# First scan of a state-space layer: two of three products with C computed by GpSimd, with their rows of C copied by ScalarE

## The reference, cut to what matters

```python
def step(h, inp):
    xt, dtt, Bt, Ct = inp
    dA = jnp.exp(dtt[:, :, None] * A)
    h = h * dA + (dtt * xt)[:, :, None] * Bt[:, None, :]
    y = jnp.einsum('bdn,bn->bd', h, Ct) + xt * D
    return (h, y)
h0 = jnp.zeros((B_, D_MODEL, D_STATE), x.dtype)
...
_, ys = jax.lax.scan(step, h0, xs)
```

## Time and profile before

| What | us |
|---|---|
| median of three runs (3369.27 to 3370.46) | 3370.19 |
| the profiled execution, its own time | 3370.55 |
| its span, first to last instruction | 3368.8 |
| VectorE busy in the span (73%) | 2445.5 |
| TensorE matmuls busy (82%) | 2766.3 |
| ScalarE busy (40%) | 1341.0 |
| GpSimd busy (18%) | 621.7 |

### The profile page before, as it was taken

One profiled execution on the slowest core, in us unless ns is written; L12 is line 12 of the kernel. 1 busy time (PEld: TensorE's weight loads), 2 busy tenths in 40 slices (PEclk: granted clock), 3 DMA queues, 4 the chain that ended last, 5 costly groups with the idle time before them and its releaser, 6 DMA issues.

```text
span 3368.8 us, 37353 instructions
## 1 busy us (share of the span) xinstructions
PE 2766.3 (82%) x12264; PEld 1579.4 (47%) x12264; DVE 2445.5 (73%) x4932; ACT 1341.0 (40%) x2454; POOL 621.7 (18%) x426
## 2 busy tenths in 40 slices
PE   4226989997898997888997989980359999999998
PEld 2003754444764444764445754440126656566564
DVE  6996687997587997687996684017767676776766
ACT  2323316763326773325772316544441131311313
POOL 2443000332100332100333000001000040310404
PEclk9558899998899998989998899995669999999999
DMA  5001000101000001000001000105010000000000
GB/s 157 0 0 45 1 1 7 26 17 52 1 1 7 23 20 53 1 1 7 23 20 52 1 1 13 26 17 118 0 33 1 1 13 1 1 13 1 14 1 13
DMA packets 57628, 65.88 MB, mean 20 GB/s; under 512 B 27756, under 2 KB 46689, under 8 KB 56801
## 3 DMA queue, kind: packets, MB, share of 16 engines
q1 hardware_dynamic: 57441, 63.51, 7.0%
HBM read 45.22 MB, written 9.88 MB: 16 GB/s over the span
## 4 chain that ended last, share of the span: by engine, by line
PE 58%; DVE 26%; issue 5%; ACT 4%; POOL 2%; DMA 1%; DVEq 1%; SPq 1%; POOLq 0%; ACTq 0%
PE psum L1713 13%; PE psum L383 8%; DVE arena L543 6%; PE psum L938 4%; PE psum L790 3%; PE psum L1773 3%; PE psum L1052 3%; DVE arena L538 3%; PE psum L956 2%; PE psum L770 2%; PE psum L373 2%; PE psum L374 2%; PE psum L269 2%; PE psum L781 2%; DVE z_both L1439 1%
## 5 line engine op out<-in xcount | busy, mean ns | idle before, releaser
L1713 PE MATMUL psum<-weights,arena 128*128 128x384 f16 x3072 | 535.3, 329 | 3.9 <-DVE arena L2069 2.9
L383 PE MATMUL psum<-arena,weights 128*128 128x512 f32 (+1 forms) x1024 | 522.6, 593 | 4.9 <-ACT arena L457 4.9
L457 ACT ACTIVATE arena<-psum,minus_scale 128x512 f32<-128x512 f32 x512 | 350.3, 685 | 215.5 <-PE psum L383 213.7
L2072 DVE SCALAR_TENSOR_TENSOR arena<-psum,arena 128x384 f32<-128x384 f32 x480 | 295.8, 616 | 193.0 <-PE psum L1713 182.6
L1713 PEld LDWEIGHTS psum<-weights,arena 128*128 128x128 f16 x3072 | 304.3, 99 | 193.3 <-issue 8.6
L598 POOL TENSOR_TENSOR arena<-arena 128x1024 f32<-128x1024 f32 x128 | 273.8, 2139 | 598.8 <-DVE arena L543 598.2
L543 DVE TENSOR_TENSOR_SCAN arena<-weights,arena 128x1026 f32<-128x1026 f32 x128 | 293.9, 2296 | 18.4 <-ACT weights L450 3.8
L246 POOL TENSOR_SCALAR shifted<-mean_var 128x4 f32<-128x4 f32 x40 | 9.7, 244 | 1313.4 <-DVE mean_var L223 1313.4
L1948 POOL TENSOR_TENSOR arena<-arena 128x512 f32<-128x512 f32 x112 | 147.5, 1320 | 510.0 <-ACT arena L1887 499.3
L383 PEld LDWEIGHTS psum<-arena,weights 128*128 128x128 f32 (+1 forms) x1024 | 166.0, 163 | 98.8 <-ACT arena L457 12.1
L450 ACT ACTIVATE weights<-arena,weights 128x512 f32<-128x512 f32 x256 | 169.2, 712 | 102.8 <-DVE arena L543 102.8
(11 more groups left out here) (322 smaller groups left out, 4880.8 us busy)
## 6 DMA issues: line engine op xcount, KB each, us to landing
arena<-arena SPq DMA_DIRECT2D x64, 128.0 KB, 2.3
arena<-head_inv SPq DMA_DIRECT2D x32, 256.0 KB, 3.4
weights<-in_qkv SPq DMA_DIRECT2D x2, 3072.0 KB, 17.4
weights<-gate_upT_kept SPq DMA_DIRECT2D x4, 1408.0 KB, 6.4
x_all<-in_x SPq DMA_DIRECT2D x4, 1024.0 KB, 12.0
weights<-in_cWkv SPq DMA_DIRECT2D x4, 1024.0 KB, 11.3
out<-x_all SPq DMA_DIRECT2D x4, 1024.0 KB, 4.4
weights<-downT_kept SPq DMA_DIRECT2D x4, 640.0 KB, 7.1
```

The lines of the kernel that those rows point to most:

```text
L383: pe.matmul(psum[0:rows, 3 + turn % 2, :], value_and_ones(kt, hd), expd[:, i % 2, :], start=kt == 0, stop=kt == NT - 1).then_inc(pv2_done, 1)
L457: a.activation(expd[:, i % 2, :], psum[:, i % 3, :], ACT.Exp, bias=minus_scale[:, :], scale=SCALE / QK ** 2).then_inc(exp_done, 1)
L1713: last = pe.matmul(psum[:, n % PROJ_BANKS, 0:W3], zT_parts[:, of_z, c, k * P:(k + 1) * P], w_parts[:, c, e, of_w, :], start=c == 0 and j == 0,
L2072: step_ = v.scalar_tensor_tensor(qkv[:, k, :], src, router_w[:, k, e:e + 1], qkv[:, k, :], ALU.mult, ALU.add)
```

## The change

In the first scan alone, 20 of the 32 products with C move from VectorE to GpSimd: those of the steps j below 30 for which j is not a multiple of 3. ScalarE copies each such row of C from PSUM into one of three SBUF buffers (`c_rows`, `keep_c`); GpSimd multiplies the state by it in place, both inputs in SBUF, and then adds (L636 and L644 of the new kernel). GpSimd no longer waits for the recurrence of the next step in the first scan. The rows of B get PSUM banks 0 to 2, the rows of C banks 3 to 7. In the loop's scans everything stays as it was. The core of the diff:

```diff
+        def b_bank(j, alone):
+            return j % 3 if alone else 5 + 2 * j % 3
+
+        def c_bank(j, alone):
+            return 3 + j % 5 if alone else 5 + (2 * j + 1) % 3
+
+        def by_pool(j, alone):
+
+            return alone and j % 3 != 0 and j < STEPS - 2
+
+        def products(upto, alone):
+
+            of_pool = sum(by_pool(j, alone) for j in range(upto))
+            return upto - of_pool, of_pool
...
-        def spread_b(pe, j):
+        def spread_b(pe, j, alone):
...
-            if j >= 2:
+            if alone and j >= 3:
+                pe.wait_ge(w_done, j - 2)
+            if not alone and j >= 2:
                 pe.wait_ge(p_done, j - 1)
...
-            if j >= 1:
+            if alone and j >= 5:
+                of_dve, of_pool = products(j - 4, alone)
+                pe.wait_ge(p_done, of_dve)
+                if of_pool:
+                    pe.wait_ge(c_row_kept, of_pool)
+            if not alone and j >= 1:
                 pe.wait_ge(w_done, j)
...
+        def keep_c(a, j):
+            i = products(j, True)[1]
+            a.wait_ge(c_psum, j + 1)
+            if i >= 3:
+                a.wait_ge(p_pool_done, i - 2)
+            a.activation(c_rows[:, i % 3, :], psum[:, c_bank(j, True), :], ACT.Copy).then_inc(c_row_kept, 1)
...
+                    if q == 0 and by_pool(j, not heads):
+                        keep_c(a, j)
...
-            v.wait_ge(c_psum, j + 1)
-            v.tensor_tensor(to[:, :, 1:], to[:, :, 1:], both(5 + (2 * j + 1) % 3), ALU.mult).then_inc(p_done, 1)
+            if not by_pool(j, alone):
+                v.wait_ge(c_psum, j + 1)
+                v.tensor_tensor(to[:, :, 1:], to[:, :, 1:], both(c_bank(j, alone)), ALU.mult).then_inc(p_done, 1)
...
-                g.wait_ge(p_done, j + 1)
-                if j + 1 < STEPS:
+                of_dve, of_pool = products(j + 1, not heads)
+                if by_pool(j, not heads):
+                    to = h[:, j % RING, :, 1:]
+                    g.wait_ge(scan_done, j + 1)
+                    if half == 0:
+                        g.wait_ge(end_kept, j + 1)
+                    g.wait_ge(c_row_kept, of_pool)
+                    row = c_rows[:, (of_pool - 1) % 3, :].unsqueeze(1).to_broadcast([P, 2, HALF])
+                    g.tensor_tensor(to, to, row, ALU.mult).then_inc(p_pool_done, 1)
+                    g.wait_ge(p_pool_done, of_pool)
+                else:
+                    g.wait_ge(p_done, of_dve)
+                if heads and j + 1 < STEPS:
                     g.wait_ge(scan_done, j + 2)
```

More of the change, by code:

```diff
@@ L207, in program @@
         Norm = namedtuple("Norm", "stat mean_var rstd shifted stats_ready shifted_ready rstd_ready")
+        p_pool_done, c_row_kept = exp_done, o_kept
         by_stage = Norm(stat, mean_var, rstd, shifted, stats_ready, shifted_ready, rstd_ready)
@@ L293, in program @@
         soft = r.take(DC, T)
+        c_rows = r.take(3, HALF)
         r = Region(arena, scan_end)
@@ L353, in spread_b, with spread_c @@
                 pe.wait_ge(split_ready, 1)
-            if j >= 2:
+            if alone and j >= 3:
+                pe.wait_ge(w_done, j - 2)
+            if not alone and j >= 2:
                 pe.wait_ge(p_done, j - 1)
-            pe.matmul(psum[:, 5 + 2 * j % 3, :], select[0:96, s, :], split[0:96, half * HALF:(half + 1) * HALF],
+            pe.matmul(psum[:, b_bank(j, alone), :], select[0:96, s, :], split[0:96, half * HALF:(half + 1) * HALF],
                       start=True, stop=True).then_inc(b_psum, 1)
-        def spread_c(pe, j):
+        def spread_c(pe, j, alone):
             s, half = j % N_STATE, j // N_STATE
-            if j >= 1:
+            if alone and j >= 5:
[4 more added lines that the diff above has]
+            if not alone and j >= 1:
                 pe.wait_ge(w_done, j)
-            pe.matmul(psum[:, 5 + (2 * j + 1) % 3, :], select[0:96, N_STATE + s, :],
+            pe.matmul(psum[:, c_bank(j, alone), :], select[0:96, N_STATE + s, :],
                       split[0:96, half * HALF:(half + 1) * HALF], start=True, stop=True).then_inc(c_psum, 1)
@@ L387, in loop_pe @@
             if scan:
-                spread_b(pe, 0)
-                spread_c(pe, 0)
-                spread_b(pe, 1)
+                spread_b(pe, 0, not heads)
+                spread_c(pe, 0, not heads)
+                spread_b(pe, 1, not heads)
             if heads:
@@ L402, in loop_pe @@
                     if scan and q == 1 and j + 1 < STEPS:
-                        spread_c(pe, j + 1)
+                        spread_c(pe, j + 1, not heads)
                     if scan and q == 3 and j + 2 < STEPS:
-                        spread_b(pe, j + 2)
+                        spread_b(pe, j + 2, not heads)
         def scan_out_pe(pe, heads):
@@ L525, in both, with scan_step @@
             return psum[:, bank, :].unsqueeze(1).to_broadcast([P, 2, HALF])
-        def scan_step(v, j):
+        def scan_step(v, j, alone):
             s, half = j % N_STATE, j // N_STATE
@@ L537, in scan_step @@
             v.wait_ge(b_psum, j + 1)
-            v.tensor_tensor(to[:, :, 1:], u[:, :, at], both(5 + 2 * j % 3), ALU.mult).then_inc(w_done, 1)
+            v.tensor_tensor(to[:, :, 1:], u[:, :, at], both(b_bank(j, alone)), ALU.mult).then_inc(w_done, 1)
             v.wait_ge(da_ready, 2 * (j + 1))
@@ L577, in loop_dve @@
                 if scan:
-                    scan_step(v, j)
+                    scan_step(v, j, not heads)
                     if j == N_STATE + 2:
```

## The result

| | us |
|---|---|
| before, median of 4 runs (3369.27 to 3370.46) | 3370.24 |
| after, median of 4 runs (3390.91 to 3397.26) | 3396.03 |
| ratio, with its 95% interval | 1.0074 (1.0062 to 1.0087) |
| profiled execution of after, its own time; its span | 3390.91; 3389.2 |

The kernel is slower by 0.74%, on the forecast side and inside the range (3378 to 3402, forecast 3392). The profiled execution is the fastest of the four.

A forecast was written before the change was run, and what follows sets the result against it. VectorE bounds the first scan; with recurrences and GpSimd operations excluding each other, turns of 186.4 us, less 4.8 for handing over, plus 1.45 at the start, give 183.1 against 161.7: 3370.55 + 21.4 = 3392 us, range 3378 to 3402.

The forecast's parts named there:

- the first rival: First scan: recurrence and GpSimd do not hold each other up; 20 products leave VectorE, 3347 us; chance 0.15.
- the open step: First scan: recurrence and GpSimd operations with two SBUF inputs assumed to exclude each other fully, though no row settles it.
- The sum: First scan, recurrences, gate product, adds and new products taking turns: 183.1 us instead of 161.7, +21.4 us.
- the handing over: First scan: each handing over to a recurrence saves 0.15 us, 4.8 in all; savings when GpSimd takes over cancel against pauses.
- pauses between GpSimd operations: First scan: 0.12 us between two GpSimd operations, let cancel against the savings when GpSimd takes over.
- the 17.2 of three steps: First scan: three recurrences and their GpSimd operations in turn want 17.2 us, against 14.9 before the change.
- The product itself: New GpSimd product in the first scan, sized from the add: 2.00 us, or 2.36 in the second buffer; 43.6 for 20.
- what follows the gate: After the first scan: keeps its length and starts later by the whole sum.
- Edits at nothing: First scan: ScalarE's 20 copies, 0.59 us each, stay covered; earlier rows of B and C win nothing.
- Partial exclusion: First scan: GpSimd delays a recurrence but waits less for one; 3368 to 3381 us; rival 2, chance 0.05.
- A dearer product: First scan: exclusion plus GpSimd product dearer than any add; over 3401 us from 0.4 us more each; rival 3, chance 0.02.

The follow-up runs named there:

- the PSUM version: The changed kernel, with VectorE writing the first scan's product with B to PSUM, where the recurrence reads it; 3350.93 us, 0.9951 of before.
- the PSUM version with three products in four: The PSUM version with three products in four on GpSimd instead of two in three (22 instead of 20); 3362.61 us, 0.9975 of before.

## Why the prediction was right

**What bounds.** VectorE was the bound of the first scan, and 20 products taken away are worth their time: the PSUM version is 24.2 us shorter in that stretch, against the 24 of the first rival's sum (its median is 19.2 us below before). That rival had the arithmetic right and the condition wrong.

**Does the recurrence belong to the operations that exclude GpSimd?** This was the open step, taken from the rows of other operations. It held: recurrences of 2.30 to 3.52 us in the changed kernel, 2.30 to 3.34 with only the wait removed, 2.29 with one input in PSUM. One of the rows it was taken from was the wrong one: the GpSimd sum of 2728.50 in the earlier trace rows began after the scalar-tensor-tensor of 2727.38. What held that one up were the two sums ahead, which end at 2728.36; 2727.38 + 2.06 - 1.22 = 2728.22 is again 0.14 us before that, so the conclusion stands:

```profile
2725.67 2.69 POOL L1948 TENSOR_TENSOR arena<-arena 128x512 f32<-128x512 f32 x2
```

The Trainium skill's rule (SBUF — State Buffer, Who interferes with whom) has now been seen for the recurrence in two parts: it names two SBUF inputs, and one in PSUM ends the wait; it names GpSimd instructions that read SBUF, and a memset passes. The Trainium skill has the other side blocked for the whole instruction (SBUF — State Buffer, SBUF: two separate sides); here either side gets in 0.14 to 0.22 us before the other's recorded end, and the measurement decides.

**The sum.** +21.4 us were forecast, 16.4 measured in the first scan. The mis-sized term is the handing over from a recurrence to GpSimd. I had let its saving of 0.14 cancel against pauses between GpSimd operations. But in the exclusive state the next GpSimd operation is already waiting, so it has no pause, and gains 0.2 us (0.22 in the add of 133.82). Three times 0.2 is 0.6 us, which takes the 17.2 of three steps to the 16.6 measured. Over some 29 recurrences it is 5.8 us; about ten pauses of 0.14 us between two adds without a recurrence in between stay (137.68 to 137.83 above), so this step accounts for 4.4 of the 5.0 us missing. The product itself was sized well: 2.17 us in every buffer of the ring (2167 to 2184 ns in the PSUM version), against 2.18 on average.

**The rest of the difference.** The forecast had what follows the gate keep its length, and nothing change ahead of the scan. That step failed: the median rose by 25.8 us, of which the first scan explains 16.4. In the profiled execution, the first recurrence starts 1.47 us later (98.23 against 96.76) although the work ahead of it is unchanged (it starts at 96.8 to 98.4 in the other profiles), and what follows the gate adds the other 2.5 of its 20.4. The remaining 5 us stand between the profiled execution and the three others. A plain delay of 18.9 us gave a median of +20.4 with runs from +16 to +21, and the 19 runs of before in that group spread over 9.4 us (3364.65 to 3374.04); which part of the three other runs has the 5 us was not profiled, and stays open. That the forecast of 3392 lies only about 4 us from the median is in part luck: 9.4 us outside the first scan, which it did not count, cover the 5.0 us by which its sum was too large.

**Edits at nothing.** The copies took 0.575 us (0.59 forecast), and neither a copy nor a decay ever ended a wait after the start. No wait of VectorE for the rows of B and C shows either.

**The other rivals.** Partial exclusion would have shown recurrences that wait while GpSimd does not; GpSimd's 3.86 and 4.2 us operations rule it out. A dearer product does not show.

The experiment with the wait alone tells something the prediction had only half seen: the wait that was dropped was worth 22 us of the first scan by itself, by letting each add run under two products with an input in PSUM. Moving twenty products saved 5.3 us of it back (183.4 to 178.1).

## What to carry to other kernels

Before moving work from VectorE to GpSimd, count the inputs in SBUF of what remains on VectorE: if it has two, and GpSimd's operation has two as well, the two took turns in every row here, and GpSimd's idle time in the profile was not there to be used. Where one of the two inputs can be written to PSUM at the same price (the product with B took 1.22 us either way), the turn-taking ended, and the move paid in full in its own stage. A wait that seems to hold an idle engine back may be what keeps it out of another's way: try its removal alone first.

## What the runs showed that I had not expected

The loop over the sequences runs the same instructions in each kernel. From the gate product of one sequence to that of the next it took 512.0 us (768.7 to 1280.7) and then 517.5 us (to 1798.2) in the changed kernel, and 518.9 us (729.0 to 1247.9) in the PSUM version with three products in four. The difference goes with TensorE's granted clock. It falls to its lower level (1.2 GHz, 0.50 of full speed) for short stretches in the same part of each turn, but not at the same places. Here is the point 122 us into the two turns of the changed kernel (busy times as above; the third figure from the right is the granted clock); TensorE is busy throughout in both:

```profile
890.70:894.10 3.40, 3.40 (x22) 2.78 (x22) 1.27 (x3) 0.37 (x1) 0.00 (x0) 1.00 0.02 5
1402.80:1406.10 3.30, 3.30 (x10) 2.42 (x10) 0.69 (x2) 0.00 (x0) 0.00 (x0) 0.50 0.02 5
```

This is one longer part, the same 282 matmuls, first in the changed kernel and then in the PSUM version with three in four:

```profile
905.70:952.60 46.90, 43.03 (x282) 37.26 (x281) 33.36 (x60) 15.83 (x26) 1.26 (x2) 0.89 0.00 1
```

```profile
868.50:919.00 50.50, 44.75 (x282) 38.20 (x282) 33.40 (x60) 15.76 (x26) 1.26 (x2) 0.84 0.00 1
```

At a mean of 0.84 instead of 0.89 the part takes 3.6 us more, and length times clock is nearly the same (42.4 and 41.7 us). Of the 6.9 us between the two turns, 2.5 lie ahead of this part and 0.8 behind it. That the clock makes the whole difference is not shown, nor what sets the places. The time of a change in front of this loop can thus differ by more than 10 us from what its own stage shows: the PSUM version with three in four has the shortest first scan of all, 1.9 us below that with two in three, and comes out 12 us slower in the median. Stages, not totals, tell such versions apart.
